# Two of sixteen states of a Mamba scan moved from the second pass to the first

## The chip, the cores and the metric

The kernel runs on one core of one Trainium2 chip. The metric is its device time in microseconds (us), less is better. A core has TensorE (PE; its weight loads are PEld), VectorE (DVE), ScalarE (ACT), GpSimd (POOL) and SyncE (SP), each with its own queue of instructions carried out in order; semaphores order them among each other. 16 DMA engines move data between DRAM and the core's SBUF.

## The reference, cut to what matters

The input x has 4096 tokens of 1024 channels.

```python
x = x + 0.5 * ffn(layernorm(x))        # ternary weights, one 1024x1024 product
x = x + mamba(layernorm(x))
x = x + 0.5 * ffn(layernorm(x))

# mamba
u, z = split(x @ W_in.T)               # 1024 channels each
u = silu(causal convolution of u over 4 tokens)
dt_r, B, C = split(u @ W_xproj.T)      # 64, 16, 16 columns
dt = softplus(dt_r @ W_dt.T + b_dt)
A = -exp(A_log)                        # [1024 channels, 16 states]
for each token t, channel d and state n:
    h[d, n] = exp(dt[t, d] * A[d, n]) * h[d, n] + dt[t, d] * B[t, n] * u[t, d]
    y[t, d] += h[d, n] * C[t, n]
y = (y + u * Dskip) * silu(z)
return y @ W_out.T
```

The recurrence is independent for each of 1024 x 16 pairs of channel and state, and sequential over the tokens. VectorE does it with tensor_tensor_scan, a chain h = a*h + b along the free axis.

## The kernel before

There are two passes, one after the other, with DRAM scratch between them.

**First pass.** It works in chunks of T1 = 512 tokens (8 of them) by 8 groups g of 128 channels. The function drive calls step(i, par, j, f_on, u_on, s_on) for each chunk i and each j of 0 to 3, and each engine has a step of its own which issues its share in a written-out order. Three chunks are in work at a time. The first layer works on chunk i + 1, one tile of 128 tokens a step: x + bias on GpSimd, row statistics on VectorE, row_scale on GpSimd, normalise on ScalarE, turn and ffn on TensorE, a high half of each turned tile on ScalarE and a low half on VectorE, into xt and xz. The u product works on chunk i, two groups g a step: product on TensorE, u_work (a copy to SBUF) on ScalarE, conv on VectorE, silu on ScalarE. The units belong to chunk i - 1. They are given in order by a list, and per_phase says how many of them each of the four phases of each step takes:

```python
units = [("y", 0), ("x", 0), ("y", 1), ("c", 0), ("d", 0), ("y", 2), ("d", 1), ("y", 3), ("d", 2), ("d", 3),
         ("y", 4), ("d", 4), ("y", 5), ("d", 5), ("y", 6), ("d", 6), ("d", 7), ("y", 7)]
per_phase = [(1, 1, 1, 1), (1, 1, 1, 2), (1, 1, 1, 1), (1, 2, 1, 1)]
```

x is the product with W_xproj (x_dbl: dt_r, B and C), c takes C, y is u * Dskip, and d is one group of dt; these d units matter here. Unit q = 8 * chunk + g takes on TensorE a product with W_dt; on ScalarE relu (L435) and abs (L436) of it, then exp (L439) and ln (L441), each of the latter with a load of its function table; on VectorE, one phase later, a chain of four instructions (L552 to L561) which ends with dt; on GpSimd dt * u (L363), called dtu; and SyncE stores dt and dtu. ScalarE's instruction L435 of unit q waits until dt of unit q - 2 is made (dt_done at q - 1). GpSimd does the d units at the end of its step.

The order of one step on ScalarE: high halves of xz, u_work of 2j - 1, normalise of the next tile of x, phase 0, silu of 2j - 1, normalise of x1, u_work of 2j, phase 1, high halves of xt, silu of 2j, phases 2 and 3. On VectorE: low halves of xz, statistics, conv of 2j - 1, x1 (L657) and its statistics, phase 0, conv of 2j, phase 1, low halves of xt, phases 2 and 3. TensorE starts a step with turn(1, ...), which waits for the low halves of xt (L508).
After the last full chunk (i = 7, 8) the first layer and then the u product are left out, so that the last chunk has units alone.

**Second pass.** It works in chunks of T2 = 256 tokens (16 of them). The body of a chunk is a loop over slots n = 0 to 15, one state each: times_b on GpSimd makes dt*u*B for 8 groups (two instructions of L1075, then L1080 adds the carried state to the first column); decays on ScalarE makes exp(dt * A) in PSUM (L1168, one instruction a group, p_da); scans on VectorE makes four scans of 128x512 (L1294) into h[n % 2]; turn_state on TensorE turns h of the state before (L1398); add_state on VectorE (L1307) and part_state on ScalarE (L1191) multiply it with C and add it up, the latter by way of adding DMAs from GpSimd's queue (L1094). Beside them each slot holds a unit of TensorE: z products (L1441), output products (L1432) or the last layer's products (L1422), and in slots 0, 4, 7 and 10 two groups of transposes (L1415) with a correction (L1452). SyncE loads B for two states at a time (load_b, L964), and dt, dtu and the rest a chunk ahead. keep_last (L1176) keeps the last column of h for the next chunk's carry.

## Time and profile before

| | |
|---|---|
| device time, median of 3 runs | 2877.55 us (2876.93 to 2884.73) |
| device time of the profiled execution | 2876.51 us |
| its span, first to last instruction | 2874.4 us |
| first pass, about | 0 to 1080 us |
| second pass, about | 1083 to 2874 us |
| busy over the span: TensorE, VectorE | 2412.2 us (84%), 2379.2 us (83%) |
| ScalarE, GpSimd | 2044.6 us (71%), 1845.6 us (64%) |
| mean granted TensorE clock | 0.921 |

Busy time of an engine is the time in which it carries out an instruction; an engine that waits on a semaphore is idle. In a timeline line the first number is the start and the second the duration, both in us, and the bracket at the end, where there is one, tells the idle time before the instruction and what ended it. L12 is line 12 of the kernel; where buffers lie in one tile under another name (rel, ex, lg, dtu are parts of "late"), the trace shows the tile's name.

### The profile page before, as it was taken

To read this page: it belongs to the slowest core of one execution; us is meant where nothing else is said; L and a number is where in the kernel's file an instruction comes from. 1 tells how busy PE (TensorE), PEld (TensorE's weight loads), DVE (VectorE), ACT (ScalarE), POOL (GpSimd) and SP (SyncE) were. 2 spreads that over 40 slices of the span, in tenths; PEclk is the share of its full clock that TensorE was granted. 3 is DMA by queue.
4 is the path that set the end of the run, shared out by engine and by line. 5 is a ranking of instruction groups with operands and counts; after the bars stand their busy time and mean duration, and the time that the engine had idled before them with its cause. 6 is when DMAs were issued, how large, how long until landed. Compare 5 with 4: busy or idle time off the path is not lost.

```text
span 2874.4 us, 37734 instructions
## 1 busy us (share of the span) xinstructions
PE 2412.2 (84%) x12448; PEld 1386.4 (48%) x12448; DVE 2379.2 (83%) x3197; ACT 2044.6 (71%) x3775; POOL 1845.6 (64%) x1449
## 2 busy tenths in 40 slices
PE   3577998998998843698998998998998998998988
PEld 1233444444443313555555555555555555555554
DVE  6556667667667556999999999999999999999992
ACT  2233667667657675788888888888888888888883
POOL 1112223222222117999999999999999999999991
PEclk8788999999999866799999999999999999999999
DMA  6553333333232337657767767766767767767744
GB/s 206 176 205 139 126 107 114 115 114 122 100 133 87 112 107 247 159 131 169 169 151 169 168 155 167 171 149 169 170 148 167 170 148 170 168 147 171 171 104 101
DMA packets 200289, 429.25 MB, mean 149 GB/s; under 512 B 44512, under 2 KB 93920, under 8 KB 199840
## 3 DMA queue, kind: packets, MB, share of 16 engines
q1 hardware_dynamic: 160928, 284.23, 29.8%
q0 software_dynamic: 39168, 142.62, 26.7%
q8 instruction: 100, 1.64, 0.2%
q14 instruction: 93, 0.76, 0.1%
HBM read 190.86 MB, written 110.10 MB: 105 GB/s over the span
## 4 chain that ended last, share of the span: by engine, by line
POOL 33%; DVE 14%; PE 8%; issue 7%; ACT 0%; DMA 0%; POOLq 0%; SPq 0%; DVEq 0%; ACTq 0%
POOL dbu L1075 25%; DVE h L1294 9%; POOL y L1094 4%; PE p_g L1432 3%; DVE y L1307 3%; PE p_ht L1398 2%; POOL y L1109 1%; PE p_g L1441 1%; POOL dbu L1080 1%; PE p_g L1422 1%; POOL x L1113 1%; DVE x L1341 0%; POOL carry L1086 0%; DVE x L1331 0%; POOL small L70 0%
## 5 line engine op out<-in xcount | busy, mean ns | idle before, releaser
L1075 POOL TENSOR_TENSOR dbu<-dtu,bb 128x1024 f32<-128x1024 f32 x512 | 1268.3, 2612 | 20.3 <-DVE h L1294 20.0
L1294 DVE TENSOR_TENSOR_SCAN h<-p_da,dbu 128x512 f32<-128x512 f32 x1024 | 1187.3, 1207 | 34.7 <-POOL dbu L1080 18.1
L1168 ACT ACTIVATE p_da<-dt,neg_a 128x255 f32<-128x255 f32 x2048 | 879.6, 467 | 243.6 <-DVE h L1294 237.9
L1398 PE MATMUL p_ht<-ident,h 128*128 128x128 f32 x4096 | 564.3, 297 | 131.5 <-DVE h L1294 130.8
L1398 PEld LDWEIGHTS p_ht<-ident,h 128*128 128x128 f32 x4096 | 513.6, 154 | 208.2 <-DVE h L1294 183.3
L1307 DVE SCALAR_TENSOR_TENSOR y<-p_ht,ct,y 128x1024 f32<-128x1024 f32 x272 | 345.1, 1269 | 19.3 <-PE p_ht L1398 19.0
L714 PE MATMUL p_u<-xz,wu 128*128 128x512 f16 x1536 | 350.0, 385 | 6.8 <-DVE xz L508 6.2
L1432 PE MATMUL p_g<-wo,tokt 128*128 128x512 f16 x1536 | 352.3, 387 | 2.9 <-ACT tokt L1211 1.6
L1441 PE MATMUL p_g<-wz,xz 128*128 128x512 f16 x1536 | 344.5, 381 | 0.0
L70 POOL TENSOR_TENSOR small<-small,consts 128x1 f32<-128x1 f32 x96 | 68.8, 717 | 423.4 <-DVE small L63 423.4
L363 POOL TENSOR_TENSOR late<-dt,u 128x512 f32<-128x512 f32 x64 | 81.6, 1274 | 376.5 <-DVE dt L561 376.5
L705 PE MATMUL p_ffn<-tern,xt 128*128 128x512 f16 x1024 | 258.3, 416 | 22.8 <-DVE xt L508 22.8
L1191 ACT ACTIVATE y_part<-p_ht,ct 128x1024 f32<-128x1024 f32 x224 | 246.5, 1100 | 33.5 <-PE p_ht L1398 29.9
L714 PEld LDWEIGHTS p_u<-xz,wu 128*128 128x128 f16 x1536 | 150.3, 99 | 199.6 <-issue 29.4
L1432 PEld LDWEIGHTS p_g<-wo,tokt 128*128 128x128 f16 x1536 | 153.4, 100 | 181.2 <-issue 17.2
L1094 POOL DMA_DIRECT2D y<-y_part x224 | 201.6, 900 | 58.8 <-issue 45.3
L1422 PE MATMUL p_g<-tern,tokt 128*128 128x512 f16 x1024 | 230.9, 379 | 3.4 <-ACT tokt L1211 2.3
L1441 PEld LDWEIGHTS p_g<-wz,xz 128*128 128x128 f16 x1536 | 151.3, 99 | 168.9 <-issue 3.2
L395 ACT ACTIVATE xn<-xin,small 128x1024 f32<-128x1024 f32 x32 | 39.7, 1241 | 238.6 <-POOL small L72 238.6
L693 PE MATMUL p_tr<-ident,xn 128*128 128x128 f32 x512 | 89.9, 333 | 124.8 <-DVE xt L508 77.7
L705 PEld LDWEIGHTS p_ffn<-tern,xt 128*128 128x128 f16 x1024 | 109.6, 107 | 161.5 <-issue 64.9
L1422 PEld LDWEIGHTS p_g<-tern,tokt 128*128 128x128 f16 x1024 | 99.5, 98 | 112.9 <-ACT tokt L1211 3.1
(118 smaller groups left out, 2805.4 us busy)
## 6 DMA issues: line engine op xcount, KB each, us to landing
y<-y_part POOLq DMA_DIRECT2D x224, 512.0 KB, 5.7
bb<-b_scratch SPq DMA_DIRECT2D x128, 256.0 KB, 4.0
xin<-in_x SPq DMA_DIRECT2D x32, 512.0 KB, 5.4
x_scratch<-x SPq DMA_DIRECT2D x32, 512.0 KB, 5.2
xz_scratch<-xz SPq DMA_DIRECT2D x16, 1024.0 KB, 6.2
y_scratch<-late SPq DMA_DIRECT2D x32, 512.0 KB, 5.4
dt_scratch<-dt SPq DMA_DIRECT2D x64, 256.0 KB, 2.1
dtu_scratch<-late SPq DMA_DIRECT2D x64, 256.0 KB, 2.4
```

The source lines that it names most:

```text
L705: mm = nc.tensor.matmul(p_ffn[h][:], xt[:, a, g, :], tern[:, g, h * HALF:(h + 1) * HALF], start=(g == 0 and a == 0), stop=(g == G - 1 and ...
L714: mm = nc.tensor.matmul(p_u[g % 2][:].rearrange("p (h t) -> p h t", h=2), wu[wa][:, kk, g * P:(g + 1) * P], xz[par][:, xa, :, kk, :], star ...
L1075: nc.gpsimd.tensor_tensor(state[:, 4 * f:4 * f + 4, :], dtu[k % 3][:], bb[n // NB % 2][:, n % NB:n % NB + 1, :].to_broadcast([P, G // 2, T2]),
L1094: pool.dma_start(into[:], part[part_of(c, n) % 3][:], accum_op=ALU.add).then_inc(done, 16)
L1168: ins_ = nc.scalar.activation(p_da[p % 2][:, k * T2 + 1:(k + 1) * T2], dt[m % NR][:, k, 1:], ACT.Exp, scale=neg_a[:, g, n:n + 1])
L1191: nc.scalar.activation(into[:], p_ht[1][:], ACT.Copy, scale=ct[par][:, 1, n:n + 1]).then_inc(y_added[1], 1)
L1294: nc.vector.tensor_tensor_scan(h[n % 2][:, 2 * p:2 * p + 2, :].rearrange("p g t -> p (g t)"), p_da[p % 2][:], dbu[n % 2][:, 2 * p:2 * p + ...
L1307: nc.vector.scalar_tensor_tensor(out=y[par][t][:], in0=p_ht[t][:], scalar=ct[par][:, t, n:n + 1], in1=y[par][t][:], op0=ALU.mult, op1=ALU. ...
L1398: mm = nc.tensor.transpose(p_ht[t][:, g * P:(g + 1) * P], h[n % 2][:, g, t * P:(t + 1) * P], ident[:])
L1422: mm = nc.tensor.matmul(p_g[b][:], tokt[:, a, g, :], tern[:, g, cols], start=(n == 0), stop=(n == 2 * G - 1))
L1432: mm = nc.tensor.matmul(p_g[b][:], tokt[:, ta, g, :], wo[:, wa, g, cols], start=(n == 0), stop=(n == 3 * G - 1))
L1441: mm = nc.tensor.matmul(p_g[b][:], xz[:, xa, g, t * P:(t + 1) * P], wz[:, wa, g, cols], start=(n == 0), stop=(n == 3 * G - 1))
```

## The change

States 4 and 10 (EARLY) are taken out of the second pass's products, decays and scans. In the first pass each d unit gets: two exponentials of dt (decay_early, ScalarE), two products dtu * B (GpSimd, straight behind dtu), two scans over 512 tokens (scan_early, VectorE, at the head of the next d unit), a copy of the last columns (keep_early, GpSimd) and two stores of h (store_early, SyncE). The decays of unit q - 1 stand in ScalarE's unit q behind relu and abs, and are written into the lg and ex tiles of unit q - 1. B of the two states is loaded back, broadcast to all partitions, once a chunk (load_early_b). The chain of dt is made in place in the dt tile. The second pass loads h of a state (load_h, 1 MB, SyncE, at the end of slots 3 and 9) into h[n % 2] for turn_state; the factor A (neg_a) is loaded and made in the first pass, and dbu buffers alternate over the fourteen scanned states.

```diff
@@ first pass, ScalarE
+                def decay_early(q):
+                    g = q % G
+                    wait(act, dt_done, q + 1)
+                    for e, n in enumerate(EARLY):
+                        nc.scalar.activation(early_da[g % 2][e], dt[g % 2][:], ACT.Exp,
+                                             scale=neg_a[:, g, n:n + 1]).then_inc(early_decay, 1)
...
                             wait(act, s_full[v % 2], d * NU + v // 2 + 1)
-                            wait(act, dt_done, q - 1)
+                            wait(act, early_scan, (q - 1) * NE)
...
                             nc.scalar.activation(rel[g % 2], p_s[v % 2][:], ACT.Relu, bias=dt_b[:, g:g + 1])
                             nc.scalar.activation(ex[g % 2], p_s[v % 2][:], ACT.Abs, bias=dt_b[:, g:g + 1]
                                                  ).then_inc(s_free[v % 2], 1)
+                            if q:
+                                decay_early(q - 1)
@@ first pass, VectorE
+                def scan_early(q):
+                    d, g = divmod(q, G)
+                    wait(dve, early_kept, q - G + 1)
+                    for e in range(NE):
+                        wait(dve, early_decay, q * NE + e + 1)
+                        wait(dve, early_product, q * NE + e + 1)
+                        nc.vector.tensor_tensor_scan(early_h[g % 2][:, e, :], early_da[g % 2][e], early_h[g % 2][:, e, :],
+                                                     early_edge[:, g, e:e + 1] if d else 0.0,
+                                                     ALU.mult, ALU.add).then_inc(early_scan, 1)
...
                         if kind == "d":
-                            wait(dve, dt_done, q)
+                            if q:
+                                scan_early(q - 1)
                             wait(dve, exp_done, q + 1)
@@ first pass, GpSimd
                         nc.gpsimd.tensor_tensor(dtu[g % 2], dt[g % 2][:], u[dpar][:, g, :], ALU.mult).then_inc(dtu_done, 1)
...
+                        wait(pool, dtu_done, q + 1)
+                        wait(pool, early_stored[g % 2], (d * (G // 2) + g // 2) * NE * 16)
+                        wait(pool, early_kept, q - 1)
+                        for e in range(NE):
+                            nc.gpsimd.tensor_tensor(early_h[g % 2][:, e, :], dtu[g % 2], early_b[:, e, :],
+                                                    ALU.mult).then_inc(early_product, 1)
+                        if q:
+                            keep_early(q - 1)
@@ second pass, SyncE
+                def load_h(c, e):
+                    n = EARLY[e]
+                    wait(sp, ht_full[1], c * NS + n - 1)
+                    wait(sp, last_kept, nth(c, n - 1))
+                    sp.dma_start(h[n % 2][:], dram["h"][bass.ds(c, 1), e].rearrange("c p g t -> p (c g) t")
+                                 ).then_inc(h_loaded[e], 16)
...
+                        if z_on and n + 1 in EARLY:
+                            load_h(i, EARLY.index(n + 1))
@@ second pass, GpSimd, ScalarE, VectorE (here GpSimd)
-                            times_b(i, par, n)
+                            if n in SCANNED:
+                                times_b(i, par, n)
@@ second pass, TensorE
                 def turn_state(c, n):
-                    wait(pe, scan_done, c * (NS * 4) + n * 4 + 4)
+                    if n in EARLY:
+                        wait(pe, h_loaded[EARLY.index(n)], (c + 1) * 16)
+                    else:
+                        wait(pe, scan_done, nth(c, n) * 4 + 4)
```

## Rows read from the trace of the kernel before

**Rows 1.** Windows: length; PE, PEld, DVE, ACT, POOL busy; clock, DMA share, GB/s.
```profile
626.00:739.00 113.00, 105.20 (x468) 50.18 (x466) 78.16 (x164) 74.50 (x96) 27.92 (x28) 0.94 0.35 117
936.00:1026.00 90.00, 69.11 (x262) 29.48 (x263) 57.53 (x100) 59.36 (x74) 11.61 (x9) 0.86 0.31 110
1026.00:1079.00 53.00, 28.38 (x63) 10.84 (x62) 24.65 (x40) 40.53 (x49) 9.27 (x8) 0.63 0.32 110
1604.00:1711.00 107.00, 96.20 (x558) 59.91 (x557) 104.93 (x116) 88.50 (x188) 101.59 (x77) 0.97 0.70 164
```

**Rows 2.** Groups by line, 1300 to 2700 us: count, then busy us, mean ns.
```profile
L1075 POOL TENSOR_TENSOR dbu<-dtu,bb 128x1024 f32<-128x1024 f32 x418 | 1036.9, 2620 | 11.5 <-DVE h L1294 11.2 <-issue 0.2
L1294 DVE TENSOR_TENSOR_SCAN h<-p_da,dbu 128x512 f32<-128x512 f32 x837 | 970.8, 1207 | 14.9 <-ACT p_da L1168 13.6 <-POOL dbu L1080 1.3
```

**Rows 3.** What TensorE waited for, 1300 to 2700 us: total, times, longest.
```profile
PE p_ht L1398 <- DVE h L1294: 50.8, 89, 1.1
PE p_g L1452 <- ACT tokt L1204: 40.0, 52, 1.3
PE p_g L1415 <- DVE x L1331: 25.6, 26, 1.5
PE p_g L1415 <- DVE q L1320: 19.7, 26, 1.1
```

**Rows 4.** DMA issues, 1300 to 2700 us: count, KB each, median us to landing.
```profile
xz<-xz_scratch SPq DMA_DIRECT2D x26, 512.0 KB, 9.2
```

**Rows 5.** Timeline of ScalarE, twice: start us, duration us, instruction.
```profile
643.94 0.67 ACT L406 ACTIVATE up<-p_u,consts 128x512 f32<-128x512 f32 x1
...
1041.70 0.67 ACT L435 ACTIVATE late<-p_s,dt_b 128x512 f32<-128x512 f32 x1
...
1044.27 0.63 ACT L439 ACTIVATE late<-late 128x512 f32<-128x512 f32 x1
...
1046.20 0.63 ACT L441 ACTIVATE late<-late 128x512 f32<-128x512 f32 x1
1046.74 0.67 ACT L435 ACTIVATE late<-p_s,dt_b 128x512 f32<-128x512 f32 x1
```

**Rows 6.** Timeline of VectorE in step 1.
```profile
644.70 0.55 DVE L519 TENSOR_SCALAR acc<-up,conv_w,conv_b 128x512 f32<-128x512 f32 x1 [5.31 <-issue]
...
647.52 0.68 DVE L544 TENSOR_TENSOR late<-p_s,dskip 128x512 f32<-128x512 f32 x1
648.12 0.42 DVE L552 TENSOR_SCALAR res<-late 128x512 f32<-128x512 f32 x1
648.57 0.69 DVE L554 TENSOR_TENSOR res<-late,res 128x512 f32<-128x512 f32 x1
...
650.71 1.28 DVE L508 TENSOR_TENSOR xt<-p_tr,xt 128x512 f16<-128x512 f32 x2
```

**Rows 7.** Timeline of GpSimd.
```profile
907.46 1.26 POOL L363 TENSOR_TENSOR late<-dt,u 128x512 f32<-128x512 f32 x1 [3.11 <-DVE dt L561]
...
929.32 1.50 POOL L363 TENSOR_TENSOR late<-dt,u 128x512 f32<-128x512 f32 x1 [11.62 <-DVE dt L561]
```

**Rows 8.** Timeline of VectorE at the same moment.
```profile
929.74 1.64 DVE L554 TENSOR_TENSOR res<-late,res 128x512 f32<-128x512 f32 x1
```

**Rows 9.** Timeline of TensorE: first transposes of steps, and x_dbl.
```profile
567.38 1.94 PE L693 MATMUL p_tr<-ident,xn 128*128 128x128 f32 x8 [2.62 <-DVE xt L508]
...
596.46 1.94 PE L693 MATMUL p_tr<-ident,xn 128*128 128x128 f32 x8 [1.57 <-DVE xt L508]
...
612.43 7.08 PE L730 MATMUL p_s<-u,wx 128*96 128x512 f32 x16 [0.89 <-ACT u L416]
...
626.17 1.04 PE L693 MATMUL p_tr<-ident,xn 128*128 128x128 f32 x8
...
651.53 1.94 PE L693 MATMUL p_tr<-ident,xn 128*128 128x128 f32 x8 [0.94 <-DVE xt L508]
...
680.22 1.16 PE L693 MATMUL p_tr<-ident,xn 128*128 128x128 f32 x8 [2.62 <-DVE xt L508]
```

More of the change, by code:

```diff
@@ L17 @@
 NS = 16
+EARLY = (4, 10)
+NE = len(EARLY)
+SCANNED = tuple(n for n in range(NS) if n not in EARLY)
 R = 64
@@ L120, in first_pass @@
         ct = sb("ct", [P, TT1, NS])
-        res = sb("res", [P, T1])
+        early_b = sb("early_b", [P, NE, T1])
+        early_h = [sb(f"early_h{i}", [P, NE, T1]) for i in range(2)]
+        early_edge = sb("early_edge", [P, G, NE])
         dt = [sb(f"dt{i}", [P, T1]) for i in range(2)]
@@ L170, in first_pass @@
         dt_stored = [sem(f"dt_stored{i}") for i in range(2)]
+        a_done, early_b_loaded, early_product = sem("a_done"), sem("early_b_loaded"), sem("early_product")
+        early_decay, early_scan, early_kept = sem("early_decay"), sem("early_scan"), sem("early_edge_kept")
+        early_stored = [sem(f"early_h_stored{i}") for i in range(2)]
+        early_da = [[lg[i], ex[i]] for i in range(2)]
         units = [("y", 0), ("x", 0), ("y", 1), ("c", 0), ("d", 0), ("y", 2), ("d", 1), ("y", 3), ("d", 2), ("d", 3),
@@ L218, in w_items, with drive @@
             return [(t, t // 8, t % 4, t % 8 >= 4) for t in range(first, first + PER_STEP)]
-        def drive(eng, step, prologue=None):
+        def drive(eng, step, prologue=None, epilogue=None):
             if prologue:
@@ L328, in step @@
                         s_stores(i - 1, j, 3)
-                drive(sp, step)
+                drive(sp, step, epilogue=store_early)
                 for b in range(2):
@@ L356, in over_partitions, with keep_early @@
                     nc.gpsimd.partition_all_reduce(whole[:, m, 1:2], whole[:, m, 0:1], P, op).then_inc(whole_done, 1)
+                def keep_early(q):
+                    wait(pool, early_scan, (q + 1) * NE)
+                    nc.gpsimd.tensor_copy(early_edge[:, q % G, :], early_h[q % 2][:, :, T1 - 1]).then_inc(early_kept, 1)
                 def s_work(d, dpar, j, phase):
@@ L500, in step @@
                         s_work(i - 1, j, 3)
-                drive(act, step, prologue)
+                    if i == 0 and j == TT1 - 1:
+                        nc.scalar.activation(neg_a[:], neg_a[:], ACT.Exp).then_inc(a_done, 1)
+                        act.wait_ge(a_done, 1)
+                        nc.scalar.mul(neg_a[:], neg_a[:], -1.0).then_inc(a_done, 1)
+                        act.wait_ge(a_done, 2)
+                drive(act, step, prologue, decay_early)
             @block.vector
@@ L677, in step @@
                         s_work(d, 1 - par, j, 3)
-                drive(dve, step, prologue)
+                drive(dve, step, prologue, scan_early)
             @block.tensor
@@ L777, in _, with second_pass @@
                 drive(pe, step, prologue)
-def second_pass(nc, sem, ins, tern, consts, ident, split_dram, dram, out):
+def second_pass(nc, sem, ins, tern, consts, neg_a, ident, split_dram, dram, out):
     with ExitStack() as ctx:
@@ L792, in second_pass @@
         wo = sb("wo", [P, 2, G, D], F16)
-        neg_a = sb("neg_a", [P, G, NS])
         carry = sb("carry", [P, NS, G])
@@ L842, in second_pass @@
         last_kept = sem("last_h_kept")
+        h_loaded = [sem(f"h_state{n}_loaded") for n in EARLY]
         ht_full = [sem(f"ht_full{t}") for t in range(TT2)]
@@ L876, in second_pass, with nth @@
         SUMMED = tuple(n for n in PARTED if n != Y2_FIRST)
+        def nth(c, n):
+            if n < 0:
+                return nth(c - 1, NS + n)
+            return c * len(SCANNED) + sum(m < n for m in SCANNED)
         def summed(c, n):
@@ L995, in prologue @@
                 def prologue():
-                    with nc.allow_non_contiguous_dma(reason="constants"):
-                        sp.dma_start(neg_a[:], ins["A_log"].rearrange("(g p) n -> p g n", p=P)).then_inc(const_loaded, 16)
                     for f in range(2):
@@ L1082, in carry_over @@
                 def carry_over(c, cpar, half):
-                    wait(pool, last_kept, c * NS + (half + 1) * (NS // 2))
+                    wait(pool, last_kept, nth(c, (half + 1) * (NS // 2)))
                     wait(pool, edge_done, c + 1)
@@ L1172, in keep_last @@
                 def keep_last(c, n):
[L1173 removed]
+                    wait(act, scan_done, nth(c, n) * 4 + 4)
                     if n % (NS // 2) == 0:
@@ L1255, in body @@
                         if z_on:
-                            decays(i, par, n, (2, 3))
+                            if n in SCANNED:
+                                decays(i, par, n, (2, 3))
                             if n - 1 in PARTED:
@@ L1359, in body @@
                     for n in range(NS):
-                        if z_on:
+                        if z_on and n in SCANNED:
                             scans(i, n, 0)
@@ L1370, in body @@
                             add_product(i, n // 10, 1)
-                        if z_on:
+                        if z_on and n in SCANNED:
                             scans(i, n, 1)
```

87 lines of the change are left out of this document (54 added, 33 removed).

## The prediction

> **What bounds the kernel now.** I read the profile in this order: busy time by stretch, then in each pass the groups by line, the waits and the timelines of one chunk. There are two regimes. In the second pass a chunk of 256 tokens takes 107.0 us (837 scans of 64 a chunk are 13.1 chunks in 1400 us [rows 2]), and in one of them VectorE is busy 104.9, GpSimd 101.6, TensorE 96.2, ScalarE 88.5 [rows 1]: VectorE and GpSimd leave nothing over, TensorE little. The first pass looks half empty: in a 113.0 us chunk of 512 tokens VectorE is busy 78.2, ScalarE 74.5, GpSimd 27.9, and only TensorE (105.2) is near full; its end has 53 us of units alone with ScalarE 40.5 busy [rows 1]. The reader is to see two different kinds of "free": a sum of idle time, and idle time that lies where an in-order queue can use it.
>
> **Second pass: what it saves.** Per chunk two states go: four products of 2.62 us, eight scans of 1.207 us [rows 2], sixteen decays and some small ones. That is 10.5 us on GpSimd (11.1 with its two 0.21 us carry additions and gaps) and 9.7 us on VectorE. If they alone set the pace, the chunk falls to about 96. TensorE does not do less: it still turns all 16 states. Its 10.9 us of idle per chunk are 3.9 behind the scans (50.8 over 13.1 chunks), 3.1 behind the hi copies (40.0) and 3.5 behind PSUM banks that VectorE empties (45.3) [rows 3]. 96.2 + 3.1 + 3.5 = 102.8 stays if only the wait on scans goes. Bounds for the saving per chunk: 107.0 - 102.8 = 4.2 and 11.1. States 4 and 10 stand in the slots where TensorE makes its two short transposes and waits for VectorE, which now reaches the bank without a scan ahead of it; following that I get about 3 us at slots 4 and 5 and 2.5 at slots 10 and 11. I take 5.5, nearer the lower bound, as 103 is where TensorE ends. 15 chunks make 82; the first chunk has no output half beside it, so GpSimd sets it and it gets some 10. Together -92, bounds -67 (16 x 4.2) and -178 (16 x 11.1).
> The h load (1 MB, twice a chunk) starts when state 2 (8) has been turned and is wanted some 9 us later; a 512 KB load lands in 9.2 [rows 4], so it may be late by a little. The b load of states 6 and 7 (12 and 13) is queued behind it on SyncE; GpSimd, freed of a state, can wait for it about 5 us a chunk before TensorE notices. At worst these eat the saving: 0 is the other bound. The neg_a load that leaves the second prologue is worth about 1: the loads behind it, the edge column's, set that start.
>
> **First pass: what it adds.** Per unit (64 in all: 8 groups of channels x 8 chunks): two exponentials on ScalarE, two products on GpSimd, two scans on VectorE, one small copy, two 256 KB stores. By sums this fits: VectorE 78.2 + 8 x 2.33 = 97 of 113, ScalarE 84, GpSimd 49. But it also ties the engines. Before, ScalarE's unit q waited only for dt of unit q - 2. Now unit q waits for the scans of q - 2, which VectorE does at the head of its unit q - 1, and in the middle of unit q stand the decays of q - 1, which wait for dt of q - 1, just made. Behind them in ScalarE's queue are ln, SiLU, both normalisations, the copy of the next u product (conv on VectorE waits for it) and the high halves (TensorE's next tile waits). On VectorE the scans of q wait for GpSimd's dt*u and two products.
> Prices. ScalarE's unit: 2.57 to its exponential, 1.93 more to the start of ln, 0.54 for ln, 5.04 in all [rows 5]; the two decays are not in the trace, by the exponential of this size 1.2 together (1.1 to 1.3 by the spacing of the reads and by its own 0.63 [rows 5]), and they take over its table load. VectorE: conv 2.8, y product 0.6, chain to dt 2.6 [rows 6], two scans 2.3 [rows 2]. GpSimd: 1.26 for a product of 128x512 [rows 7], so dt*u and two products end 3.9 after dt. Whether the scans run beside those products: VectorE's difference of two SBUF tiles took 1.64 instead of 0.69 when it started inside a GpSimd product [rows 6, 7, 8]. The new scans read both operands from SBUF (the second pass's read their decays from PSUM), so I make them wait for the second product: scans end at dt + 6.3, next dt at dt + 8.9. With full overlap it would be dt + 7.8; that is the lower price.
> This is where the Trainium skill speaks against the change ("SBUF — State Buffer", section "SBUF: two separate sides"): a VectorE instruction with two SBUF inputs and a GpSimd instruction that reads SBUF exclude one another for a whole instruction. By that rule the scans can't overlap the products, 8.9 a unit; without it 7.8, and the first pass would come out about 38 us shorter. No row here shows it for a scan.
>
> One full chunk by hand, in us from the start of its step 1 (626.17 [rows 9]), with the short durations (x + bias 2.35, row_scale 1.3, normalise 1.15, SiLU with its table 1.9, statistics 1.6) off the same timelines. The copy of u product 2 moves from 17.8 [rows 5] to 19.0; conv, y, scans, chain: dt0 at 28.1, and step 2 starts at 28.9 (before 25.4). dt1 = dt0 + 8.9 = 37.0. dt2: ScalarE ends unit 2 at 40.8, then xz high and low 42.6, statistics, conv, x1, statistics 50.4, scans, chain: 55.3. dt3: ScalarE's decays start only at dt2, so ln ends at 59.1, SiLU, normalise and copy at 62.7, then conv, y, scans, chain: 71.2; step 3 starts at 72.0 (before 54.1). dt4 = 80.1. dt5: products and x + bias keep GpSimd to 86.5, row_scale 88.8, normalise 90, unit 5 at 96.2, SiLU, normalise, copy 99.8, conv, y, scans, chain: 108.3. ScalarE's unit 6 again waits for it: ln at 112.1, xt halves, step 0 at 113.5 (before 83.1). dt6 = 118.8, dt7 = 127.7. Then products, x + bias, row_scale, normalise, SiLU: x_dbl on TensorE at 138.6, and from there 13.7 to the next step 1 as before (612.43 to 626.17): 152.3, against 112.8 (567.38 to 680.22) [rows 9]. The rise per step is 3.5, 14.4, 12.4 and 9.1: 39.4 a chunk, and six chunks have this form: +236. Bounds: 34.8 with overlapped scans (+209); 46 if TensorE, now idle 47 us of each chunk, runs x_dbl and a u product at its lower clock (+276; they ran so after idle stretches, with 0.63 granted in the last 53 us [rows 1]).
> Chunk 7 (u product and units, no first layer, 90 us [rows 1]): the same timetable without normalisations, from x_dbl to x_dbl, gives +31. The last (units alone, one each 5.04 us, ScalarE's own pace [rows 5]): 1.2 + 7 x (8.9 - 5.04) = +28. End: one more decay, product, scan and store, +5. First pass +236 + 31 + 28 + 5 = +300, bounds +262 (209 + 28 + 20 + 5) and +340.
> Costed at nothing: the stores and b loads, about 5 MB a chunk more where the pass moves 13 MB (117 GB/s x 113 us) with its DMA engines 0.35 busy [rows 1], so about half busy afterwards; if that cover were gone they would hold early_h and with it GpSimd's products. The exponential of neg_a, once, is 2 us in a step that waits for weights.
>
> **Sum.** The profiled execution: span 2874.4, its own time 2876.5, 1.0 under the median of 2877.55. 2876.5 + 300 - 92 - 1 = 3083.5, and 1.0 for the median: 3085. Own range of this case: down by the 38 of overlapped scans and by 45, half the way to the second pass's far bound, 3000; up by the 40 of the low clock, 25 to the near bound and 20 for late loads of h and b, 3170.
>
> **Rivals.**
> (A) The idle time takes the work (other side, faster). ScalarE's waits for dt fall in its own idle time, and TensorE, 105 of 113 busy, goes on setting the first pass. For it: all sums fit, and VectorE stands idle for 5.3 us before a conv [rows 6]. Against it: those waits are for ScalarE's copy, which is itself pushed back. It decides if the decays find dt ready, that is if a chunk stays under 112.8 + 92/6.5, about 127. Time: 2876.5 + 5 - 92 + 20 (the last chunk, where ScalarE has no idle time) = 2810. Chance 0.09.
> (B) Half: the coupling costs only in steps 2 and 3 where two units follow without other work, about 18 a chunk, +108, + 45 in chunks 7 and 8, + 5: 2943. For it: steps 0 and 1 have slack in every queue; against: each of them starts late by what ScalarE lost before. Chance 0.13.
> (C) The second pass saves nothing, as the h load and the b load behind it are late on TensorE and GpSimd: 3177. For it: DMA engines 0.70 busy [rows 1], both loads behind a wait in one queue; against: the 9 us of lead. Chance 0.09.
> Forecast as worked out: 0.69.
>
> **How the numbers follow.** Below 2950 lie A and half of B (0.15), above 3170 a part of C (0.05): the range is 2950 to 3170. A change within 0.3% (9 us) is about what a measurement of this kernel can't tell from none. Faster is A, 0.09; the same needs A's and B's costs to cancel the saving, 0.02; slower 0.89.
>
> **What would show it.** Right: a first-pass chunk near 152 with TensorE under 75% busy; ScalarE's largest new wait its decays or its first unit instruction, behind VectorE's dt or scans; GpSimd to scan to dt cycles near 9 us in the last 70 us; scans of over 1.2 us, or a gap, beside products; second-pass chunks near 101.5 with TensorE's wait for scans smaller. Wrong: a first-pass chunk under 130 (ScalarE waits in its idle time), second-pass chunks at 96 (TensorE has more room than I say) or at 107 (h or b late). The forecast hangs most on one step, that ScalarE's queue passes the delay of dt on to conv and to TensorE's next tile.

## The result, and the profile after

| | before | after |
|---|---|---|
| device time, median of 4 runs each, side by side | 2881.14 us (2876.93 to 2885.97) | 3178.34 us (3176.09 to 3182.08) |
| ratio, 95% interval | | 1.1032 (1.1008 to 1.1057) |
| profiled span | 2874.4 us | 3174.3 us |
| second pass begins (first instruction of VectorE's prologue) | 1083.5 | 1388.2 |
| length of the second pass | 1790.9 | 1786.1 |
| mean granted clock | 0.921 | 0.892 |

The first pass grew by 304.8 us (forecast +300). The second gave back 4.9 (forecast -92). The sum lies within 2 us of rival (C)'s number, 3177, and 8 us above the range.

First pass, TensorE's timeline: x_dbl, which stands once in a chunk [rows 9].
```profile
733.20 7.08 PE L801 MATMUL p_s<-u,wx 128*96 128x512 f32 x16 [1.88 <-ACT u L461]
885.84 7.08 PE L801 MATMUL p_s<-u,wx 128*96 128x512 f32 x16 [1.41 <-ACT u L461]
1036.99 3.22 PE L801 MATMUL p_s<-u,wx 128*96 128x512 f32 x7 [1.88 <-ACT u L461]
```
A chunk takes 152.6 and 151.2 here. Below, "the first-pass chunk" is the mean of the four periods between the second and the sixth x_dbl: 111.6 before, 152.4 after. (The expectations below were written with single periods and say 111.7 and 152.8.)

The first transposes of the steps of one chunk, the same view.
```profile
746.93 1.04 PE L764 MATMUL p_tr<-ident,xn 128*128 128x128 f32 x8
...
776.74 1.94 PE L764 MATMUL p_tr<-ident,xn 128*128 128x128 f32 x8 [0.18 <-DVE xt L567]
...
820.14 1.94 PE L764 MATMUL p_tr<-ident,xn 128*128 128x128 f32 x8 [4.51 <-DVE xt L567]
...
860.85 1.94 PE L764 MATMUL p_tr<-ident,xn 128*128 128x128 f32 x8 [5.57 <-DVE xt L567]
...
899.57 0.60 PE L764 MATMUL p_tr<-ident,xn 128*128 128x128 f32 x4
```
From the start of step 1 the next ones start at 29.8, 73.2, 113.9 and 152.6; the timetable in the prediction said 28.9, 72.0, 113.5 and 152.3.

The units alone, in three timelines of one cycle. VectorE:
```profile
1364.48 3.35 DVE L595 TENSOR_TENSOR_SCAN early_h<-late,early_edge,early_h 128x512 f32<-128x512 f32 x2 [2.82 <-POOL early_h L405]
1367.76 0.40 DVE L625 TENSOR_SCALAR dt<-late 128x512 f32<-128x512 f32 x1
...
1369.71 0.69 DVE L632 TENSOR_TENSOR dt<-dt,late 128x512 f32<-128x512 f32 x1
```
GpSimd:
```profile
1361.74 1.27 POOL L398 TENSOR_TENSOR late<-dt,u 128x512 f32<-128x512 f32 x1 [3.84 <-DVE dt L632]
1363.09 2.49 POOL L405 TENSOR_TENSOR early_h<-late,early_b 128x512 f32<-128x512 f32 x2
1365.52 1.12 POOL L391 COPY early_edge<-early_h 128x2 f32<-128x2 f32 x1
1370.48 1.29 POOL L398 TENSOR_TENSOR late<-dt,u 128x512 f32<-128x512 f32 x1 [3.84 <-DVE dt L632]
```
ScalarE:
```profile
1361.77 1.33 ACT L467 ACTIVATE late<-dt,neg_a 128x512 f32<-128x512 f32 x2
...
1367.93 0.69 ACT L487 ACTIVATE late<-p_s,dt_b 128x512 f32<-128x512 f32 x1 [2.37 <-DVE early_h L595]
```
The reader is to see the order of one turn: dt, then dt*u and the products, then the scans, then the next dt, 8.74 us in all (1361.74 to 1370.48; forecast 8.9). The first scan starts when the first product is done, not the second, but the pair of scans then takes 3.35 us (2.18 and 1.25, which overlap a little); where GpSimd is idle a pair takes 2.45. ScalarE's pair of decays takes 1.33 (forecast 1.2), and its first unit instruction waits for the scans. In the full chunks it does so too; waits from 567 to 1000 us, as total, times, longest:
```profile
ACT late L487 <- DVE early_h L595: 54.2, 16, 6.1
```

Second pass. What the engines waited for, 1700 to 2800 us, as total, times, longest. Before, the last of them had 50.8 in 1400 us [rows 3], and GpSimd had no wait for B from 1300 to 2700 us.
```profile
PEld p_ht L1484 <- DVE h L1377: 95.8, 77, 3.4
POOL dbu L1159 <- DMA bb<-b_scratch: 82.7, 13, 10.2
PE p_ht L1484 <- DVE h L1377: 62.0, 71, 2.9
```
Timeline of SyncE in one of those waits:
```profile
1995.15 0.32 SPq L1063 DMA_DIRECT2D h<-early_h_scratch  x1
1995.53 1.04 SPq L1034 DMA_DIRECT2D y<-y_scratch  x2
1996.61 0.73 SPq L1040 DMA_DIRECT2D bb<-b_scratch  x1
```
and of GpSimd:
```profile
2004.78 4.67 POOL L1159 TENSOR_TENSOR dbu<-dtu,bb 128x1024 f32<-128x1024 f32 x2 [4.46 <-DMA bb<-b_scratch]
```
B is in 8.2 us after its load was issued (1996.61 to 2004.78), behind the 1 MB of h and two loads of y; GpSimd has stood idle for it for the last 4.46. From 1700 to 2800 us the median load of B takes 6.9 us from issue to landing, against 3.9 before. h itself is in time: TensorE waits for it 0.3 us in 1200. How such a stretch looks in windows of 5.36 us (columns as in [rows 1]):
```profile
1780.84:1786.20 5.36, 5.36 (x29) 2.57 (x27) 4.71 (x5) 3.61 (x7) 5.01 (x4) 1.00 1.01 300
1786.20:1791.56 5.36, 4.27 (x35) 3.48 (x34) 2.10 (x3) 3.53 (x8) 0.41 (x2) 1.00 1.00 280
```
The DMA engines are full (1.01 and 1.00), and in the second window GpSimd is busy 0.41 of 5.36 us and VectorE 2.10. Full windows alone are nothing new: before has some of 1.02 and 1.05 (1583.90 and 1632.14), with GpSimd busy for 4.93 and 5.00.

### The profile page after: what moved, and what is told of

It is laid out like the page before. It is cut to its first block, busy times and chain, and to the rows that moved or that the text cites. A ratio compares the mean times of both kernels' runs of the same rounds, so it can differ in the third digit from the quotient of the medians.

```text
span 3174.3 us, 37962 instructions
## 1 busy us (share of the span) xinstructions
PE 2435.6 (77%) x12448; PEld 1383.2 (44%) x12448; DVE 2445.5 (77%) x3197; ACT 2020.6 (64%) x3617; POOL 1891.9 (60%) x1545
## 4 chain that ended last, share of the span: by engine, by line
POOL 23%; DVE 13%; issue 9%; PE 6%; ACT 4%; DMA 1%; SPq 0%; POOLq 0%; DVEq 0%; ACTq 0%
POOL dbu L1159 18%; DVE h L1377 9%; DVE y L1390 3%; PE p_ht L1484 2%; PE p_g L1518 2%; POOL y L1178 2%; POOL y L1193 1%; ACT p_da L1249 1%; ACT y_part L1272 1%; POOL dbu L1164 1%; PE p_g L1527 1%; DVE x L1414 1%; PE p_g L1508 1%; POOL x L1197 1%; ACT tokt L1292 1%
## 5 line engine op out<-in xcount | busy, mean ns | idle before, releaser
L1159 POOL TENSOR_TENSOR dbu<-dtu,bb 128x1024 f32<-128x1024 f32 x448 | 1109.0, 2631 | 136.1 <-DMA bb<-b_scratch 134.2
L1377 DVE TENSOR_TENSOR_SCAN h<-p_da,dbu 128x512 f32<-128x512 f32 x896 | 1041.9, 1207 | 148.5 <-ACT p_da L1249 80.0
L1249 ACT ACTIVATE p_da<-dt,neg_a 128x255 f32<-128x255 f32 x1792 | 770.4, 468 | 297.9 <-DVE h L1377 295.2
L1484 PE MATMUL p_ht<-ident,h 128*128 128x128 f32 x4096 | 542.2, 290 | 174.3 <-DVE h L1377 172.1
L1484 PEld LDWEIGHTS p_ht<-ident,h 128*128 128x128 f32 x4096 | 494.4, 150 | 249.7 <-DVE h L1377 224.8
L785 PE MATMUL p_u<-xz,wu 128*128 128x512 f16 x1536 | 364.1, 396 | 38.3 <-DVE xz L567 35.0
L1390 DVE SCALAR_TENSOR_TENSOR y<-p_ht,ct,y 128x1024 f32<-128x1024 f32 x272 | 344.9, 1268 | 36.7 <-PE p_ht L1484 36.4
L1518 PE MATMUL p_g<-wo,tokt 128*128 128x512 f16 x1536 | 343.5, 380 | 9.8 <-ACT tokt L1292 8.8
L764 PE MATMUL p_tr<-ident,xn 128*128 128x128 f32 x512 | 97.1, 352 | 161.9 <-DVE xt L567 104.2
L595 DVE TENSOR_TENSOR_SCAN early_h<-late,early_edge,early_h 128x512 f32<-128x512 f32 x112 | 162.0, 1486 | 56.8 <-POOL early_h L405 54.7
```

The lines of the kernel that those rows point to most:

```text
L785: mm = nc.tensor.matmul(p_u[g % 2][:].rearrange("p (h t) -> p h t", h=2), wu[wa][:, kk, g * P:(g + 1) * P], xz[par][:, xa, :, kk, :], star ...
L1159: nc.gpsimd.tensor_tensor(state[:, 4 * f:4 * f + 4, :], dtu[k % 3][:], bb[n // NB % 2][:, n % NB:n % NB + 1, :].to_broadcast([P, G // 2, T2]),
L1249: ins_ = nc.scalar.activation(p_da[p % 2][:, k * T2 + 1:(k + 1) * T2], dt[m % NR][:, k, 1:], ACT.Exp, scale=neg_a[:, g, n:n + 1])
L1377: nc.vector.tensor_tensor_scan(h[n % 2][:, 2 * p:2 * p + 2, :].rearrange("p g t -> p (g t)"), p_da[p % 2][:], dbu[s % 2][:, 2 * p:2 * p + ...
L1390: nc.vector.scalar_tensor_tensor(out=y[par][t][:], in0=p_ht[t][:], scalar=ct[par][:, t, n:n + 1], in1=y[par][t][:], op0=ALU.mult, op1=ALU. ...
L1484: mm = nc.tensor.transpose(p_ht[t][:, g * P:(g + 1) * P], h[n % 2][:, g, t * P:(t + 1) * P], ident[:])
```

## The experiments

All start from the changed kernel. Those without an interval are single runs. In the tables "chunk 1" is the first-pass chunk, "pass 2 at" the second pass's beginning, "chunk 2" the mean of 14 second-pass chunks, by GpSimd's carry (L1086 before, L1170 after). Before they are 111.6, 1083.5, 107.2; after 152.4, 1388.2, 107.1.

### B ahead of h on SyncE (e1_b_first)
```diff
-                        if z_on and n + 1 in EARLY:
-                            load_h(i, EARLY.index(n + 1))
...
                                 load_b(i + 1, 0)
+                        if z_on and n in EARLY:
+                            load_h(i, EARLY.index(n))
```


> The changed kernel with one thing moved: SyncE issues the h load behind the load of B for the next pair of states instead of ahead of it. First pass unchanged (chunk 152.8, end near 1388). Theory (B is late because it stands behind the h load and its wait): GpSimd's 134 us of waits for B fall under 20, a second-pass chunk goes from 107.1 to about 101.5, total about 3178 - 15 x 5.6 - 5 = 3090. Rival 1 (TensorE, ScalarE and VectorE hold one another at 107 whatever GpSimd does): the waits for B go and others take their place, chunk 106 to 107, 3165 to 3180. Rival 2 (GpSimd and VectorE alone set the pace): chunk 96 to 97, about 3010.

3170.13 us (3155.66 to 3177.32, 4 runs), ratio 1.0993 (1.0957 to 1.1029) to the kernel before; chunk 1 152.2, pass 2 at 1389.2, chunk 2 106.4. The wait has changed its owner; the same view and stretch as above:
```profile
POOL dbu L1159 <- DVE h L1377: 60.8, 52, 2.8
...
PE p_ht L1484 <- DMA h<-early_h_scratch: 23.2, 10, 3.6
```
GpSimd waits for B 9.9 us in these 1100 instead of 82.7, but TensorE waits for h. The order alone is worth 0.7 a chunk here, and 1.1 to 1.2 in the three later runs that keep full h loads behind B (105.9 to 106.0); the expected 3090 was wrong.

### ScalarE's start wait undone (e2_start)
```diff
-                            wait(act, early_scan, (q - 1) * NE)
+                            wait(act, dt_done, q - 1)
...
                             wait(act, exp_done, q + 1)
+                            wait(act, early_scan, (q - 1) * NE)
                             nc.scalar.activation(lg[g % 2]
...
-early_da = [[lg[i], ex[i]] for i in range(2)]
+early_da = [[early_a[i], lg[i]] for i in range(2)]
```
With B ahead of h.

> As e1, and in the first pass the start of ScalarE's unit q waits for dt of q - 2 again, as in the kernel before, not for the scans of q - 2: one of the decays gets a tile of its own (y0 has one buffer for that), the other stays in lg and ln waits for its scan. The decays still wait for dt of q - 1. Theory (the decays' wait for the dt just made is what stalls ScalarE): a first-pass chunk stays within 2 us of 152.8, as the unit's 2.6 us up to its decays end about when that dt comes. Rival (the wait at the unit's start does it): under 142.

3161.25 us; chunk 1 151.9, pass 2 at 1387.3. The wait that the unit's first instruction gained costs nothing by itself: ScalarE then stands at the decays instead, as its waits from 600 to 900 us show:
```profile
ACT late L468 <- DVE dt L634: 41.8, 12, 6.1
```
The run has one buffer for y0 where the change has two; that costs nothing either.

### Decays that wait for nothing (e3_decays)
```diff
-                    wait(act, dt_done, q + 1)
...
-                        nc.scalar.activation(early_da[g % 2][e], dt[g % 2][:], ACT.Exp,
+                        nc.scalar.activation(early_da[g % 2][e], dskip[:], ACT.Exp,
```
These lines come on top of the run before; both decays go to tiles of their own, and wait for the scans of two units back.

> As e2, and the decays of the first pass read Dskip instead of dt and wait for no dt, both into tiles of their own (Dskip and B of the early states are cut to half their size, so h of the two states and y0 of half the channels aren't the reference's; the work on each engine stays the same). The h loads of the second pass bring an eighth of h (128 KB). Theory (ScalarE's wait is most of the 40 us a chunk, GpSimd's products the rest): chunk 120 to 132. Rival (the products and the port shared with GpSimd are most of it): over 142. Second pass: chunk no more than 1 us under e1's, if the size of the h load no longer matters once B goes first; if DMA bandwidth is short, 2 us or more under it.

3064.83 us; chunk 1 143.9, pass 2 at 1339.2, chunk 2 102.8. The first pass missed the expectation of 120 to 132 and fell in its rival's range (over 142): this wait is worth 8.5 a chunk. In the units alone the turn stays at 8.74. The second pass, with h loads of 128 KB, dropped by itself to 102.8; that was the first sign of its cause.

### Products that wait for nothing (e4_products)
```diff
+                        for e in range(NE):
+                            nc.gpsimd.tensor_tensor(early_h[g % 2][:, e, :], u[dpar][:, g, :], early_b[:, e, :],
+                                                    ALU.mult).then_inc(early_product, 1)
                         wait(pool, dt_done, q + 1)
```


> The changed kernel, but in the first pass GpSimd's two products take u instead of dt*u (h of the two states isn't the reference's) and are issued ahead of the wait for dt, so that a scan waits for no product of its own dt. ScalarE's waits as in the changed kernel. Theory: the stretches from one dt to the next that GpSimd sets (0 to 1, 3 to 4, 6 to 7, and the two x + bias behind products) lose 2.5 to 3 each: chunk 138 to 143, and the units alone go from 8.75 to about 6. Rival (products are most of the cost): under 128. Second pass: h loads of 128 KB, still ahead of B. If the size of the h load makes B late, chunk near 102; if its wait in SyncE's queue does, 105 to 107.

3087.92 us; chunk 1 147.8, pass 2 at 1359.9, chunk 2 103.0 with h still ahead of B. Again less than expected: 4.5 a chunk, and the units alone take 8.15 a turn where about 6 was expected. Neither the theory nor its rival (under 128) holds.

### Both, all work kept (e5_work_only)
The two edits above together, with h loads of full size and B ahead of h.

> The decays of e3 (Dskip in place of dt, no wait for it) and the products of e4 (u in place of dt*u, ahead of the wait for dt) together: all the added work of the first pass, but neither ScalarE nor GpSimd makes it wait for dt. Outputs as in e3 and e4 aren't the reference's. The h loads of the second pass are full, B first, as in e1. The theory of the forecast (the added waits make the 40 us a chunk): chunk 115 to 125 (before 111.7, after 152.8). Rival, after e3 gave back only 9 and e4 only 5: the two scans themselves stand ahead of each chain of dt on VectorE, 2.3 to 3.3 us x 8 units on the chain from dt to dt, and that no waits can take away: chunk 135 to 141.

3072.3 us; chunk 1 136.9, pass 2 at 1293.9, chunk 2 106.0. With neither decays nor products waiting for dt, a chunk is still 25 above before, as the rival (the scans' own time ahead of dt) had it. The coupling alone, as I had stated it then, has fallen.

But "all work kept" does not mean that the work takes the same time. Products that no longer stand behind dt run beside the chain that makes the next dt, and both sides get longer. One instruction of the chain in the units alone (1208 to 1290 us), by count, busy us, mean ns:
```profile
L628 DVE TENSOR_TENSOR dt<-late,dt 128x512 f32<-128x512 f32 x8 | 12.1, 1519 | 0.3
```
and the same one as changed (1300 to 1386 us):
```profile
L627 DVE TENSOR_TENSOR dt<-late,dt 128x512 f32<-128x512 f32 x8 | 5.5, 692 | 0.3
```
In the units alone a turn takes 8.15 us (two of the last seven 7.74), not much less than 8.74: the ring of waits is open, and the turn is nearly as long. In a full chunk VectorE is busy for 110.7 us instead of 104.3 and GpSimd for 57.7 instead of 52.4, with the same instructions. So 15.4 is what the waits are worth after this loss; without the loss they may be worth more, which no run shows.

### Decays and scans moved later (e6_later)
```diff
                             nc.scalar.activation(lg[g % 2], ex[g % 2], ACT.Ln, bias=1.0).then_inc(ln_done, 1)
+                            if q:
+                                decay_early(q - 1)
...
                             nc.vector.tensor_tensor(res[:], res[:], rel[g % 2], ALU.add).then_inc(dt_done, 1)
+                            if q:
+                                scan_early(q - 1)
```
(and no longer at their old places).

> A kernel that computes the reference, made to beat the changed one: B first in the second pass; in the first pass the decays of q - 1 stand behind ln of q on ScalarE and the scans of q - 1 behind the chain of dt of q on VectorE, so that dt waits for neither (one decay has a tile of its own, y0 one buffer). If the scans ahead of the chain are the cause: chunk 118 to 130, total about 3170 - 6 x 28 - 15 = 2985. If it is the waits whatever their place, or the sum of VectorE's and GpSimd's work on one port: chunk 140 or more, total over 3090. In either case over before's 2883, since the second pass gives at most 30 back.

3194.83 us (3190.11 to 3198.75, 4 runs), ratio 1.1087 (1.1069 to 1.1106); chunk 1 155.5. Nothing is left out here, and it is slower than the change. The scans, all but those of the first chunk:
```profile
L597 DVE TENSOR_TENSOR_SCAN early_h<-late,early_edge,early_h x112: 1254/2066/2257, 482.9 to 1407.8; 128x512 f32<-128x512 f32 x112
...
  ACT L495: 171.2, 47
```
Minimum, median and maximum are in ns. The scans of one unit now stand beside dt*u and the products of the next: of a pair the first takes mostly 1.28 us and the second 2.2, and the median of all is 2.07. In the changed kernel the same line reads:
```profile
L595 DVE TENSOR_TENSOR_SCAN early_h<-late,early_edge,early_h x112: 1251/1266/2178, 473.6 to 1384.1; 128x512 f32<-128x512 f32 x112
```
And ln (L495) waits for them, 171.2 us in all. GpSimd loses as well, which is the greater surprise. Its dt*u by count, busy us, mean ns, here:
```profile
L399 POOL TENSOR_TENSOR late<-dt,u 128x512 f32<-128x512 f32 x64 | 129.9, 2030 | 415.6 <-DVE dt L633 415.6
```
and as changed:
```profile
L398 POOL TENSOR_TENSOR late<-dt,u 128x512 f32<-128x512 f32 x64 | 81.6, 1274 | 489.2 <-DVE dt L632 489.2
```
Its products (L406) have a median of 2.06 us instead of 1.27. Out of VectorE's way to dt, the scans stand in the way of ScalarE's ln and of GpSimd's products.

### Short scans, all waits kept (e8_short_scans)
```diff
-nc.vector.tensor_tensor_scan(early_h[g % 2][:, e, :], early_da[g % 2][e], early_h[g % 2][:, e, :],
+nc.vector.tensor_tensor_scan(early_h[g % 2][:, e, 0:8], early_da[g % 2][e][:, 0:8], early_h[g % 2][:, e, 0:8],
```


> The changed kernel, but each scan of the first pass covers 8 columns instead of 512 (h of the two states isn't the reference's); all waits stay, B first and h loads of 128 KB in the second pass. Rival of e5 (the scans' own time ahead of the chain): 2.3 to 3.3 us less for each of 8 units, chunk 126 to 134, units alone from 8.75 to about 6.5. Theory of the forecast (the waits of ScalarE and GpSimd): chunk 143 to 150. Second pass as in e3, 102.8 a chunk.

3001.06 us; chunk 1 137.2, pass 2 at 1272.7, chunk 2 102.9. 15.2 a chunk: between the two expectations. The scans' time counts as much as all the waits for dt, and the two overlap: once the waits are gone, short scans are worth 11.3 (below). The units alone take 6.84 a turn (about 6.5 expected).

### Small h loads alone (e9_small_h)
```diff
-sp.dma_start(h[n % 2][:], dram["h"][bass.ds(c, 1), e].rearrange("c p g t -> p (c g) t")
+sp.dma_start(h[n % 2][:, 0:1, :], dram["h"][bass.ds(c, 1), e, :, 0:1].rearrange("c p g t -> p (c g) t")
```


> The changed kernel with one edit: each h load of the second pass fetches one group of channels (128 KB) instead of eight (1 MB); the turned tile keeps other numbers in the other groups, so y is another. Order, waits and counts stay. Theory (the size of the h load delays B, dt, xz and the rest on the same DMA engines; its wait ahead of the b load costs nothing): second-pass chunk 102.8 to 103.2 instead of 107.1, B landing in about 4 us, and the whole kernel at 3178 - 15 x 4.2 = 3113 (3105 to 3120); the first pass stays at 1388. Rival (the wait of h ahead of the b load on SyncE): chunk stays above 105.5, kernel above 3150. Rival 2 (in the earlier runs with small h loads, the lighter first pass had left something behind that helped): 104 to 105.5.

3115.31 us; pass 2 at 1388.2, chunk 2 102.8, span 3113.5. This is the expected 3113: the size of the h loads costs 4.3 us a chunk and 61 us in all, with h still ahead of B. It is a single run, but all eight runs with small h loads have second passes of 1721 to 1731 us. The waits for B shrink, but do not go, and its median load takes 5.6 us, not the expected 4:
```profile
POOL dbu L1159 <- DMA bb<-b_scratch: 41.1, 20, 3.9
PE p_ht L1484 <- DVE h L1377: 39.5, 66, 1.4
```
With these waits of up to 3.9 us a chunk takes 102.8; with those of up to 10.2 it took 107.1.

### Short stores (e11_short_stores)
```diff
+                        w = T2 if g == 0 else 8
-                        sp.dma_start(dram["h"][bass.ds(d * 2, 2), e, :, g].rearrange("h p t -> p h t"),
+                        sp.dma_start(dram["h"][bass.ds(d * 2, 2), e, :, g, 0:w].rearrange("h p t -> p h t"),
-                                     early_h[g % 2][:, e, :].rearrange("p (h t) -> p h t", h=2)
+                                     early_h[g % 2][:, e, :].rearrange("p (h t) -> p h t", h=2)[:, :, 0:w]
```


> The changed kernel with small h loads, and the first pass stores h in full for the first group of channels alone, 16 columns for the seven others; h is not kept, the rest is computed. The forecast costed these stores (4 MB a chunk) at nothing. Theory (they cost nothing, the chain on the engines sets the first pass): chunk 152 to 153, second pass starts at 1386 to 1389. Rival (the stores hold early_h, and so GpSimd's products): chunk under 148. The second pass as in the run with small h loads.

3122.26 us; chunk 1 152.6, pass 2 at 1390.9, chunk 2 103.2. The stores cost the first pass nothing, though they are 4 MB a chunk, as the prediction had it.

### One edit after another: no waits, short scans, short decays, short products
The run of both edits (e5_work_only), then in addition scans of 8 columns (e10_no_waits), decays of 8 columns (e12_short_decays), and products of 8 columns in six of eight groups (e13_short_products). The second adds to the first
```diff
-nc.scalar.activation(early_da[g % 2][e], dskip[:], ACT.Exp,
+nc.scalar.activation(early_da[g % 2][e][:, 0:8], dskip[:, 0:8], ACT.Exp,
```
and the third
```diff
+                            w = T1 if g < 2 else 8
-nc.gpsimd.tensor_tensor(early_h[g % 2][:, e, :], u[dpar][:, g, :], early_b[:, 0, :],
+nc.gpsimd.tensor_tensor(early_h[g % 2][:, e, 0:w], u[dpar][:, g, 0:w], early_b[:, 0, 0:w],
```


> The kernel in which decays read a constant tile and products read u, neither behind dt (e5_work_only), and now also the scans of the first pass work on 8 columns instead of 512, and h loads are small: the recurrence of states 4 and 10 is not computed. Decays, products and stores keep their full size. The first pass's chunk was 152.8 as changed, 137.0 with the waits for dt gone, 137.3 with short scans alone, and 111.6 before. Theory (they are separate stretches of one chain, dt to products to scans to the next dt, and take the time one after the other): 121 +- 3, and what remains above 111.6 is the decays' time in ScalarE's queue, 8 x 1.2 = 9.6. Rival (they overlap, one hides behind the other, and something else holds the pass at 137, such as the products or stores): 130 to 137. Rival 2 (nothing remains): 112 to 116.

> As the run without waits and with short scans (first-pass chunk 126.1), and the two decays of a unit also work on 8 columns instead of 512: neither decay nor recurrence of states 4 and 10 is computed, products and stores keep their size. 14.5 us a chunk stand open against the 111.6 of the kernel before. Theory (the decays' own time in ScalarE's in-order queue): the pair takes 1.34 at full size and an estimated 0.4 at 8 columns, so 8 x 0.9 = 7.5 fewer, a chunk of 118 to 119.5. Rival (ScalarE hides them, the rest sits in GpSimd's products or in the small instructions): above 123.

> As the run with short decays, and the products of six of the eight groups work on 8 columns too (the other two stay full, so that every buffer has been written); states 4 and 10 are not computed at all. Theory (GpSimd has the room for its products; only the two short copies and overheads remain): within 1.5 us of the run with short decays, 116.5 to 119. Rival (the products, 2.5 us a unit, delay GpSimd's first-layer work at the end of its step, and with it ScalarE's normalise): 6 x 2.2 = 13 fewer at most, 106 to 114.

| | time, us | chunk 1 | step |
|---|---|---|---|
| as changed | 3178.34 | 152.4 | |
| no waits for dt | 3072.3 | 136.9 | -15.4 |
| and short scans | 2918.31 | 125.6 | -11.3 |
| and short decays | 2899.72 | 121.8 | -3.8 |
| and short products | 2847.74 | 116.1 | -5.7 |
| kernel before | 2881.14 | 111.6 | -4.5 |

(The steps are of chunk 1. The second row has B ahead of h; from the third on the h loads are small too, which takes 55 us from the second pass, 1776.6 to 1721.2, but does not reach the first.) None of the three came out in an expected range. Short scans gave 125.6, between 121 +- 3 and 130. With short decays too the chunk stayed at 121.8, above the expected 118 to 119.5 and under the rival's 123. GpSimd's products, for which I had expected 1.5 at most, are worth 5.7; their rival had up to 13. The steps hold for this order of edits only. Neither of the two sharp pictures holds: the 40.7 us are no single wait and no single engine. Windows of 600 to 900 us show what the chunk gets back; as changed:
```profile
600.00:900.00 300.00, 214.36 (x886) 101.15 (x884) 207.05 (x351) 167.05 (x217) 104.75 (x104) 0.84 0.33 113
```
with short products:
```profile
600.00:900.00 300.00, 265.22 (x1178) 128.15 (x1178) 211.63 (x448) 195.93 (x280) 89.79 (x129) 0.95 0.43 144
```
TensorE's share goes from 71% to 88% and its granted clock from 0.84 to 0.95, while VectorE's share hardly moves. The clock has a part in the 40.7 that the table does not show: for the same work TensorE is busy for 103.1 us a chunk before (clock 0.94) and 109.9 as changed (0.83 to 0.84). How much of these 6.8 us lies on the path no run tells.

## Why the prediction was right and wrong

**Right: the first pass, by its timetable.** +304.8 was measured where +300 stood. By its terms: six full chunks +233.4 (from first to seventh x_dbl 900.97 against 667.56; forecast 236), chunk 7 +36.7 (116.85 against 80.20; forecast 31), the last chunk and end +31.3 (90.0 against 58.7; forecast 28 + 5), and 3.4 ahead of the first x_dbl, which I had not counted. The terms miss by -2.6, +5.7, -1.7 and +3.4, so a part of the nearness of the sum is luck. The step rises of 3.5, 14.4, 12.4 and 9.1 came out as 4.4, 14.7, 13.0 and 9.0 (after: 29.8, 43.4, 40.7, 38.7; before: 25.4, 28.7, 27.7, 29.7). So the queues were followed rightly. Sums of busy time, by which "this fits", were no guide: as changed no engine is busy for more than 72% of the 300 us shown above. Rivals (A) and (B) are out.

**Right sum, cause told too narrowly.** "The forecast hangs most on one step, that ScalarE's queue passes the delay of dt on". The run without ScalarE's wait for dt is only 8.5 a chunk faster, and with the products' wait gone too 15.4. Another 20.8 went with the length of scans, decays and products, work that stands in order in three queues at once. The timetable held this, since it counted scans and products in every cycle, but the sentence did not. How the 40.7 divide between waits, work and instructions that make one another longer stays open, as the runs without waits have more of the last. Of the remaining 4.5 (short instructions, copies, what is left of the products) I have no run.

**Right: the lock.** The scans' pair took 3.35 us beside the products against 2.45 beside an idle GpSimd, and the cycle came to 8.74 for 8.9 (by full overlap 7.8). The first scan did not wait for the end of the second product, as I had it; it ran beside it and lost the time in its own duration. The Trainium skill's rule ("SBUF — State Buffer", section "SBUF: two separate sides"), that a VectorE instruction with two SBUF inputs and a GpSimd instruction that reads SBUF exclude one another, agrees with this (the slow scan ends 1.08 us after the second product, and takes 1.25 to 1.27 alone) and with the median scan of 2.07 us in the run with decays and scans moved later. The prediction had priced it once, as scans that wait for products; that GpSimd's instructions lose too (2.19 us instead of 1.27 for dt*u in that run, by the medians) it had not.

**Wrong: the second pass, -92.** It gave -4.9. The step that failed is "GpSimd, freed of a state, can wait for it about 5 us a chunk before TensorE notices", and with it the value 5.5 chosen between 0 and 11.1; the range allowed 20 us for late loads. Two things were mis-sized.

First, the loads. GpSimd waited for B 82.7 us in 1100, 8 a chunk, in 13 waits of up to 10.2. With h loads an eighth as large and nothing else changed, the second pass fell from 1786.1 to 1725.3: of the 87.1 missing, 60.8 are the size of the h loads. That it is the size and not the place ahead of B is shown by the exchange of the two, which moved the wait to h and gave 0.7 a chunk (1.2 at most). Rival (C), to which I gave 0.09, named this mechanism; that its number was met to 2 us is partly luck, since late loads account for 60.8 us and not for all 92. I had argued against it by the lead of h, which was in time; late was B behind it. The row to be asked was another than the one I used, how long B's own load takes: 3.9 us before, 6.9 after. The 9.2 us of a 512 KB load [rows 4] would not have given it, as the 1 MB of h itself landed in a median of 6.9. The sign of being wrong that the prediction gave for this, chunks at 107 with h or b late, is what came.

Second, the saving without late loads is 4.4 a chunk, not 5.5 (15 x 1.1 = 16.5), and the first chunk gave 0.3 in that run, not 10 (69.7 against 70.0 to its carry; 68.6 as changed). 60.8 + 16.5 + 9.7 = 87.0 of 87.1. Why the first chunk gave nothing, though GpSimd has two states less in it too, stays open.

The bound of 102.8 was met (102.6 to 103.2 in the eight runs with small h loads), but not for my reason. Sums over 11 chunks, before:
```profile
sum 1178.87, PE 1058.72 PEld 662.20 DVE 1147.89 ACT 974.97 POOL 1107.94; mean PE 96.25 PEld 60.20 DVE 104.35 ACT 88.63 POOL 100.72
```
with small h loads:
```profile
sum 1130.36, PE 1021.76 PEld 628.94 DVE 1046.88 ACT 896.96 POOL 998.31; mean PE 92.89 PEld 57.18 DVE 95.17 ACT 81.54 POOL 90.76
```
as changed:
```profile
sum 1178.21, PE 1042.82 PEld 648.43 DVE 1051.07 ACT 898.54 POOL 997.92; mean PE 94.80 PEld 58.95 DVE 95.55 ACT 81.69 POOL 90.72
```
I had said that TensorE stays busy for 96.2 and loses the 3.9 of its wait for the scans. That wait stayed (39.5 us in 1100 with small h loads; 50.8 in 1400 before [rows 3]); its idle time fell by 1.0 a chunk (10.9 to 9.9) and its busy time by 3.4, with a granted clock of 0.98 to 1.00 in each chunk instead of 0.95 to 0.97. As changed, busy time fell by 1.5 and idle time rose by 1.4 (10.9 to 12.3), which is no gain: VectorE and GpSimd have 8.8 and 10.0 us a chunk less to do, and all of it is spent on waiting.

## What to carry to other kernels

Work moved into a stretch whose engines look half empty is to be laid into each in-order queue by hand before it is called free: here the sum said it fits, the timetable said +39.4 a chunk, and +40.7 came. Taking a wait away, or moving work behind it, is no gain by itself: see what the freed instructions then run beside, and whether both keep their length. A large load costs by its size in the queue that it shares: look at what small load stands behind it and how long its reader can wait, not at the large one's own lead. And an engine at 96 of 107 us is already the bound, so that taking 9 to 10 us from the two fuller ones buys at most what its waits and its clock give back.

## What was not expected of the hardware

A GpSimd copy of two columns (L391) took 1.12 us while VectorE scanned two SBUF operands, and mostly 0.19 where the scans were short. Counts, busy us and mean ns over 600 to 900 us, as changed:
```profile
L391 POOL COPY early_edge<-early_h 128x2 f32<-128x2 f32 x16 | 8.6, 538 | 0.0
```
with short scans and no waits:
```profile
L393 POOL COPY early_edge<-early_h 128x2 f32<-128x2 f32 x21 | 3.9, 187 | 0.0
```
In the second pass of before, TensorE's clock fell in single places of a chunk, behind a stretch with idle time. Windows of 5.36 us of before:
```profile
1546.38:1551.74 5.36, 4.05 (x28) 2.73 (x26) 5.36 (x7) 4.67 (x11) 5.27 (x5) 1.00 0.92 179
1551.74:1557.10 5.36, 3.28 (x15) 2.45 (x16) 5.36 (x6) 5.09 (x11) 5.28 (x5) 0.83 0.41 107
1557.10:1562.46 5.36, 5.36 (x27) 3.31 (x26) 4.23 (x5) 5.16 (x12) 5.01 (x5) 0.85 0.29 97
```
A granted clock of 0.83 or 0.85 means that the window is spent partly at 1.2 GHz and the rest at 2.4; another such window of that chunk has 0.68. Idle time alone does not foretell it: windows of the same chunk with TensorE busy for 3.51 and 3.14 us read 1.00. With small h loads all twenty windows of 5.14 us in one chunk read 1.00. The 3.4 us of busy time that go with it are most of what the second pass gains there. They come in two parts. From before to as changed, with two states fewer on VectorE, TensorE's busy time falls by 1.5 a chunk, and the clock of eleven chunks is 0.95 to 1.00, mostly 0.97; from there to small h loads, with nothing else changed, it falls by another 1.9. Through which wait each part comes is not shown.
